# A graph attention layer on one core: slots of a word side by side, the maximum subtracted on VectorE, one exponent for four heads

## The reference

```
xl, xr = (h @ Wl), (h @ Wr)                      # (1250, 4, 64), h = rms(layernorm(x)) @ W_down
msg = xl[src] + xr[dst]
e = einsum(where(msg > 0, msg, 0.2 * msg), att)  # one number for each edge and head
m = segment_max(e, dst); p = exp(e - m[dst])
alpha = p / (segment_sum(p, dst) + 1e-16)
out = segment_sum(alpha * xl[src], dst) @ W_up
```

## Time and profile before

| what | value |
|---|---|
| three runs | 1125.25 us median (1120.89 to 1125.56) |
| the profiled execution | 1124.86 us, span 1122.3 us |
| mean granted TensorE clock | 0.931 |
| busy: PE, DVE, POOL, ACT | 970.0, 956.2, 616.1, 528.2 us |
| moved by transfers | 105.30 MB, 94 GB/s |

### The profile page before, as it was taken

One profiled execution on the slowest core, in us unless ns is written; L12 is line 12 of the kernel. 1 busy time (PEld: TensorE's weight loads), 2 busy tenths in 40 slices (PEclk: granted clock), 3 DMA queues, 4 the chain that ended last, 5 costly groups with the idle time before them and its releaser, 6 DMA issues.

```text
span 1122.3 us, 10318 instructions
## 1 busy us (share of the span) xinstructions
PE 970.0 (86%) x2998; PEld 465.6 (41%) x2998; DVE 956.2 (85%) x1078; ACT 528.2 (47%) x1901; POOL 616.1 (55%) x657
## 2 busy tenths in 40 slices
PE   0798999999999998999999999998999947566754
PEld 0675544444574343444344444443444423222321
DVE  6989648492999999999999999899997387888795
ACT  0123213311666677667878878767776121111111
POOL 2323327446666666676777777767762264444332
PEclk9899999999969999999999999998999967867788
DMA  8104051244343432553355333573320100000001
GB/s 255 76 1 119 10 181 34 51 142 139 100 155 80 155 83 77 158 160 98 87 156 171 84 82 91 208 280 81 91 79 22 61 1 0 38 19 19 20 37 52
DMA packets 59462, 105.30 MB, mean 94 GB/s; under 512 B 24631, under 2 KB 32468, under 8 KB 59130
## 3 DMA queue, kind: packets, MB, share of 16 engines
q0 software_dynamic: 18560, 50.70, 16.2%
q1 hardware_dynamic: 40842, 53.92, 14.4%
HBM read 92.30 MB, written 12.45 MB: 93 GB/s over the span
## 4 chain that ended last, share of the span: by engine, by line
DVE 48%; PE 32%; issue 10%; POOL 4%; SPq 2%; ACT 1%; DMA 1%; POOLq 0%; DVEq 0%; ACTq 0%
PE acc L715 25%; DVE acc_sb L1428 11%; DVE z L1558 7%; DVE round_mem L1556 7%; DVE round_mem L1419 4%; PE acc L888 3%; DVE round_mem L1174 3%; DVE round_mem L1175 2%; DVE round_mem L1173 2%; POOL round_mem L666 2%; PE acc L886 2%; POOL round_mem L490 1%; DVE round_mem L1172 1%; DVE big_b L1496 1%; DVE big_b L1372 1%
## 5 line engine op out<-in xcount | busy, mean ns | idle before, releaser
L666 POOL DMA_INDIRECT round_mem<-msg_table,idx x352 | 338.0, 960 | 99.9 <-issue 88.8
L1109 ACT ACTIVATE round_mem<-round_mem,pz 128x66 f32<-128x66 f32 x1408 | 345.1, 336 | 2.0
L715 PE MATMUL acc<-wslot,big_a 128*128 128x512 f32 x512 | 225.1, 600 | 4.4 <-issue 2.1
L1428 DVE TENSOR_REDUCE acc_sb<-round_mem 128x264 f32<-128x1848 f32 (+1 forms) x62 | 206.2, 3326 | 5.9 <-ACT round_mem L1109 3.8
L490 POOL TENSOR_TENSOR round_mem<-round_mem 128x1024 bf16<-128x1024 bf16 (+3 forms) x52 | 85.6, 1653 | 132.6 <-DVE round_mem L1176 87.7
L715 PEld LDWEIGHTS acc<-wslot,big_a 128*128 128x128 f32 x512 | 97.9, 193 | 127.5 <-issue 123.1
L715 PE MATMUL acc<-big_a,xhat_t 128*128 128x512 f32 x320 | 139.9, 600 | 6.5 <-ACT xhat_t L1039 5.0
L1102 ACT ACTIVATE pz<-z 128x7 f32<-128x7 f32 (+1 forms) x248 | 55.5, 296 | 148.3 <-DVE z L1565 105.7
L1419 DVE TENSOR_TENSOR round_mem<-round_mem,tp 128x1536 f32<-128x1536 f32 (+1 forms) x62 | 103.4, 1668 | 25.3 <-issue 19.8
L715 PE MATMUL acc<-wslot,big_b 128*128 128x512 f32 x256 | 113.1, 601 | 8.9 <-DVE big_a L1375 6.3
L715 PE MATMUL acc<-big_b,wslot 128*128 128x512 f32 x256 | 110.0, 592 | 0.0
(11 more groups left out here) (195 smaller groups left out, 1159.7 us busy)
## 6 DMA issues: line engine op xcount, KB each, us to landing
big_b<-in_x SPq DMA_DIRECT2D x18, 512.0 KB, 10.9
round_mem<-msg_table,idx POOLq DMA_INDIRECT x352
out_x<-big_b SPq DMA_DIRECT2D x9, 512.0 KB
wslot<-in_wv_t SPq DMA_DIRECT2D x2, 2048.0 KB
wslot<-in_wk_t SPq DMA_DIRECT2D x2, 2048.0 KB
wslot<-in_wo_t SPq DMA_DIRECT2D x2, 2048.0 KB
wslot<-in_wq SPq DMA_DIRECT2D x2, 2048.0 KB
wslot<-in_gate_w SPq DMA_DIRECT2D x1, 2048.0 KB
```

The costliest lines, as they stand in the source:

```text
L666: pool.indirect_dma_start(xg[g % 4][:, j, :], None, msg_table, bass.IndirectOffsetOnAxis(idx[:, c, j0 + j:j0 + j + 1], 0)).then_inc(xg_in[ ...
L715: mm = nc.tensor.matmul(o(acc[:, n % 4, :]), a, b, start=first, stop=last)
L1109: ins = nc.scalar.activation(xg[g % 4][:, j, cols], xg[g % 4][:, j, cols], ACT.Copy, scale=pz[:, g % 2, j, h:h + 1])
L1428: nc.vector.tensor_reduce(acc_sb[:, c, :], xg[g % 4][:, 0:n + 1, :].rearrange("p j f -> p f j"), AX.X, ALU.add).then_inc(sum_done, 1)
```

## The change

- **Weighted slots in an own buffer.** `round_mem` loses one slot of each `xg` buffer and `beside`, `msum`; it gains three half buffers (`weighted`, `halves_of`), in which a word's slots stand side by side. ACT's multiplications and POOL's `rescale` write there with a step of 7 words; `close` reads it in one piece. A round needs two of the three halves, so ACT waits between heads 1 and 2 for `sum_done` of the round before.
- **65 words for a head.** The linear part becomes word 0 of a head in `msg_table` and in `xr_sb`, so that adding the receiver adds it too and one sum over 65 words gives the score. `complete` on POOL, `beside`, `lin_done` and DVE's L1560 go. Slots that a node doesn't have now gather the row `NOBODY`, whose linear part is large (`far_col`).
- **PSUM.** `m4` lies in PSUM (`turned`, over four banks); the receiver is copied there by DVE at the first round of a chunk (`receiver`); `att` is read from SBUF. `show_receivers` and its waits go.
- **The maximum.** DVE subtracts the new maximum from the round's scores, and ACT takes one `Exp` over all slots and heads.
- **Order.** `gather(0)` is issued between pieces; `rescale(g - 3)` stands after the fourth gather of round g; a gather waits for `mul_done` only. Piece 11 is turned after `("p", 3)`. DVE enters the rounds on `wq_taken` 12 and not on the stores; those are waited for by ACT and POOL in round 0. The planner's clock becomes `268.0, 8.4`.

```diff
-ROUND_0_AT, ROUND_STEP = 286.0, 9.6
+ROUND_0_AT, ROUND_STEP = 268.0, 8.4
-                ("gram", 15): 8, ("p", 1): 9, ("p", 2): 10, ("p", 4): 11}
+                ("gram", 15): 8, ("p", 1): 9, ("p", 2): 10, ("p", 3): 11}
...
+        xg = [round_mem[0:NC, i * R * ROW:(i + 1) * R * ROW].rearrange("p (j f) -> p j f", j=R) for i in range(4)]
+        weighted = round_mem[0:NC, 4 * R * ROW:].rearrange("p (i f j) -> p i f j", i=3, j=R + 1)
+        halves_of = [weighted[:, 0:2], weighted[:, 2::-2], weighted[:, 1:3]]
...
+        turned = ps("turned", [P, 4 * HALF])
+        receiver = turned[0:NC, 0:H * MR].rearrange("p (h d) -> p h d", d=MR)
+        m4 = turned[0:NC, 4 * HALF - R * H * MR:].rearrange("p (j h d) -> p j h d", j=R, d=MR)
...
+            def gather(g):
+                c, j0, n, _, _ = ROUNDS[g]
+                if g >= 4:
+                    pool.wait_ge(mul_done, g - 3)
+                for j in range(n):
+                    if j == 4 and g >= 3:
+                        rescale(g - 3)
+                    pool.indirect_dma_start(xg[g % 4][:, j, :], None, msg_table,
+                                            bass.IndirectOffsetOnAxis(idx[:, c, j0 + j:j0 + j + 1], 0)).then_inc(xg_in[g % 4], 16)
...
+                    if q == 10:
+                        pool.wait_ge(idx_done, 1)
+                        pool.wait_ge(table_out, 16)
+                        gather(0)
                     leave_piece(q)
...
-        early = {index_of["p", i]: 273.0 + 3 * i for i in range(3)}
+        early = {index_of["p", i]: 257.0 + 2 * i for i in range(3)}
...
                 act.wait_ge(z_done, g + 1)
-                if first and 1 <= c < C - 1:
-                    show_receivers(c + 1)
+                nc.scalar.activation(pz[:, g % 2, 0:slots + 1, :], z[:, g % 3, 0:slots + 1, :], ACT.Exp, scale=-1.0).then_inc(e_done, 1)
+                act.wait_ge(e_done, g + 1)
                 for h in range(H):
-                    ins = nc.scalar.activation(pz[:, g % 2, 0:slots + 1, h], z[:, g % 3, 0:slots + 1, h], ACT.Exp, scale=-1.0,
-                                               bias=z[:, (g + 1) % 3, top_slot(g + 1), h:h + 1])
+                    if h == H // 2:
+                        if g >= 1:
+                            act.wait_ge(sum_done, g)
...
+                    to = halves_of[g % 3][:, h // 2, (h % 2) * MR:(h % 2 + 1) * MR, :]
+                    for j in range(slots):
+                        ins = nc.scalar.activation(to[:, :, j], xg[g % 4][:, j, h * HR + 1:(h + 1) * HR], ACT.Copy, scale=pz[:, g % 2, j, h:h + 1])
                 ins.then_inc(mul_done, 1)
...
-                nc.vector.tensor_reduce(acc_sb[:, c, :], xg[g % 4][:, 0:n + 1, :].rearrange("p j f -> p f j"), AX.X, ALU.add).then_inc(sum_done, 1)
+                nc.vector.tensor_reduce(running[c].rearrange("p (i f) -> p i f", i=2), halves_of[g % 3][:, :, :, 0:n + 1], AX.X,
+                                        ALU.add).then_inc(sum_done, 1)
...
-            for w in wt_out:
-                dve.wait_ge(w, 16 * 6)
+            dve.wait_ge(wq_taken, 12)
...
-                nc.vector.tensor_reduce(top, zz[:, 0:slots + 1].rearrange("p j h -> p h j"), AX.X, ALU.min).then_inc(z_done, 1)
+                step(nc.vector.tensor_reduce(top, zz[:, 0:slots + 1].rearrange("p j h -> p h j"), AX.X, ALU.min))
+                nc.vector.tensor_tensor(zz[:, 0:slots + 1], zz[:, 0:slots + 1], top.unsqueeze(1).to_broadcast([NC, slots + 1, H]),
+                                        ALU.subtract).then_inc(z_done, 1)
```

More of the change, by code:

```diff
@@ L288, in gps_layer @@
         gnn_out = [xr_sb[:, c, 0:HID] for c in range(C)]
-        xr_ps = [tp[0:NC, c % 2, 0:HID] for c in range(C)]
-        att_ps = tpb[0:NC, 0, 0:2 * HID].bitcast(F32)
+        running = [acc_sb[:, c, 0:H * MR] for c in range(C)]
         gnn_nat = [acc_sb[:, c, 0:HID] for c in range(C)]
```

145 lines of the change are left out of this document (56 added, 89 removed).

## The result

| what | before | changed |
|---|---|---|
| 20 runs each, beside each other | 1125.55 us median (1120.89 to 1130.78) | 1129.49 us median (1123.18 to 1133.85) |
| profiled execution | 1124.86 us, span 1122.3 | 1129.47 us, span 1127.3 |
| busy from 240 to 880: PE, DVE, ACT | 616.9, 586.6, 432.5 us | 614.7, 512.9, 398.0 us |
| rounds entered | 280.35 | 278.05 |
| last product of PE ends | 877.9 | 882.7 |

The ratio is 1.0041, 95% interval 1.0025 to 1.0056: a little slower. The forecast was 1125.0, faster or no change rather than slower. Later executions of the same changed kernel were far slower still (medians of 1159 to 1165 us); the experiments come to that.

The account below looks back on a forecast made before the run. PE bounds, following DVE's rounds up to its last gap: round 35 at 566, product taken at 569.5, 44 groups of 7.0 us end at 877.7, with the tail untouched 1125 us; range 1108 to 1146.

Parts of the forecast that it names:

- a 6-slot round: DVE's instructions for one round without a product: from 9.21 us to 7.87.
- PSUM at nothing: DVE reading and writing `m4` in PSUM: no added time; upper bound +1.2 us for each of three instructions.
- ACT didn't pace: Rival, chance 0.14: ACT's stepped multiplications pace the rounds from 0.31 us each; at 0.33 the time is 1140 us.
- the start: Between weight pieces and rounds: earlier first gathers, PE waiting 6.0 us for piece 10, rounds begun at 269.8, not 280.35.
- the flag and the jump: DVE before the rounds: 0.8 us for the flag, the jump at the low end of 1.24 and 5.39 us.
- The last wait for `t1`: PE's last gap, before the eleventh `t1` group: ACT takes `t1` 6 in round 35, at 569.5 us.
- The 44 groups behind it: PE's groups after the last gap: 7.0 us each, 308 us, ending at 877.7.
- the two gates that I held equal: PE's waits for `t1` 6 (round 35) and `base` 4 (behind round 60): the same end within 1 us.
- none behind 570: PE's timeline: gaps of about 1.5 us in `kv` and early `t1`, and no gap after 570 us.
- 1119.5 to 1130.5: The range in us of the likeliest case, same time within 0.5%.
- the likeliest case: Same time within 0.5%, chance 0.40: the plan takes products in later rounds, so PE's gaps stay, 21.8 against 22.0 us.
- POOL's rival: Slower, chance 0.05: a stepped write makes `rescale` take twice its time, 8.7 us a round, 1135 us.

Follow-up runs that it names:

- e1: The changed kernel with the planner's two old numbers (286 and 9.6): 1122.87 us, 0.9986 of the kernel before.
- e15: The changed kernel with one gather less in each round from round 4 on and the old plan (286 and 9.6): 1109.55 us, 0.9899 of the kernel before.
- e4: The kernel before with the new plan (268 and 8.4), nothing else: 1202.89 us, 1.0709 of the kernel before.
- e14: The changed kernel with one gather less in each round from round 4 on, new plan: 1128.79 us, 1.0062 of the kernel before.
- e6: The changed kernel with unused slots gathering 30 different padding rows, not one: 1160.29 us, 1.0332 of the kernel before.
- e7: The changed kernel with unused slots spread over 30 rows and the old plan (286 and 9.6): 1125.73 us, 1.0032 of the kernel before.
- e13: The changed kernel unedited, the control of the fourth group: 1165.14 us, 1.0382 of the kernel before.
- e5: The changed kernel unedited, run again in the second group: 1160.37 us, 1.0353 of the kernel before.
- e12: The changed kernel with scaled messages laid slot after slot as before, not side by side: 1212.77 us, 1.0810 of the kernel before.
- e11: The kernel before with unused slots gathering the last row, one small DVE instruction more: 1122.07 us, 1.0001 of the kernel before.
- e16: The kernel before with one gather more in each round: 1193.06 us, 1.0629 of the kernel before.
- e3: The changed kernel with the first round's six gathers moved back behind the last two weight pieces: 1154.51 us, 1.0275 of the kernel before.

## Why the prediction was wrong

**Right, by its own steps.** `close` 2.05 and 1.78 us (forecast 2.05 and 1.78); a 6-slot round 7.85 (7.87); PSUM at nothing; the receiver's copy 0.43; ACT's cadence 0.25 and its one exponent 0.23, so ACT didn't pace; the wait for `sum_done` cost nothing, though ACT stood 39.8 us in it; PE bounds, and DVE's 74 us less are worth nothing behind the last gate. The subtraction, at 0.226 us, was 0.2. On PSUM: the sum (L1548) had no operand there before and takes 1783 ns for 1753, with 24 elements more, which at 1.04 ns make 25 of the 30. The Trainium skill (VectorE: DVE Perf Modes, The TRN2 errata) would by my sum have added 0.2 us a round, and the rows don't show it. That sum was too large in any case: it counted three instructions, and two of them had an operand in PSUM before.

**The step that failed is the start.** I had "first instruction of the rounds at 269.8", with 274 as the high end; it was 278.05. The 8.25 us are, within 0.1: the first gather 1.2 late (250.5 for 249.3); the six gathers 2.05 more (9.45 for 7.4), which I had priced from rows where DVE ran other work; PE's next group 1.7 and the turns 0.6 more at the lower clock, which I hadn't priced at all; and 2.8 in the flag and the jump, 4.9 us for the 2.1 that I took, at the low end of my two rows.

Put through my sum, that is the miss of the first runs, and it shows a second size that was off, the other way. The last wait for `t1` should have ended at about 569.5 and ended at 577.0, 7.5 later. The 44 groups behind it took 302.5 us and not 308, since a group that waits for nothing takes 6.88 us (110.1 for the last 16) and not my 7.0. And of the two gates that I held equal within a microsecond, `base` 4 was the later one, by 3.2 us, so "none behind 570" fell: 577.0 + 302.5 + 3.2 = 882.7, for 877.7. That 1129.5 lies inside my 1119.5 to 1130.5 is thus partly luck: with the right price of a group I would have said some 1119.5, and missed by 10. The sign, slower, is the start's and the gate's.

**The mechanism held.** A group waits for a round that the plan names, and the new plan names later ones. I had said so and taken it as the likeliest case, but left the old plan aside as a comparison. With 286 and 9.6 and the short rounds, e1's expectation had no gap but piece 10's and an end at 868 to 870; e15, with a sixth of the gathers missing, shows just that, at 859.6. The new numbers cost the long rounds 78 us (e4) and the short ones 19 (e14 to e15) to 35 (e6 to e7). So what the shorter rounds save goes into the new plan, and nothing is left over.

**What no step held: the crawls, and a stop of ACT.** POOL's rival had a chance of 0.05 for a slow `rescale`, which was wrong in kind. The gathers did become the limit, but through PE and ACT: e13 to e14, with a sixth of the gathers left out, is 36 us. Between the first runs (1129.5) and e5 (1160.4) lie 31 us, and 4 of them are something else. In round 1 ACT's exponent is done at 292.7 in e5, and its multiplications start at 298.2:

```profile
292.50 0.23 ACT L1092 ACTIVATE pz<-z 128x28 f32<-128x28 f32 x1 [0.98 <-issue]
298.18 4.01 ACT L1103 ACTIVATE round_mem<-round_mem,pz 128x65 f32<-128x65 f32 x16 [5.45 <-remote]
```

DVE (4.51 us) and POOL (2.86) stand with it, the first `close` comes at 298.2 and not at 294.1, and p0 begins at 318.1 and not at 314.1. At the same place DVE and POOL stand until 295.5 to 300 in all fifteen later traces of the changed kernel and its variants, e12, e14 and e15 among them, which have no crawl. The changed kernel's first trace lacks it, and so do the kernel before, e4, e11 and e16. What ACT waits for there isn't shown.

**Open.** The first runs of the changed kernel (20, median 1129.5) have no crawl in their trace, though POOL issues 75 gathers from 272 to 372 and 146 from 543 to 748 with no pause over 0.8 us there, more in a row than in any trace that crawls, and p0 takes 24.3 us:

```profile
314.11 24.30 PE L717 MATMUL acc<-colsum,wslot 128*128 128x1 f32 x128 [0.76 <-DVE big_b L1366]
```

The same kernel crawled in each of three later groups, each on another chip. So dense gathers go with the crawls in every pair that I ran, but something else, which no run here shows, decides whether they come. It could be the chip, or where things lay in its memory; that is a guess, and no run here tests it. The stop of ACT in round 1 sets the first trace apart from the later ones too, crawls or not. What PE and ACT wait for in them isn't shown either. Nor is the start taken by itself: e3 moves it, with crawls on top. A version faster than both that leaves nothing out wasn't found; e1 (0.9986, its interval holds 1) is the nearest.

## What to carry to other kernels

Where work is placed by a table of due times, put the old table through with the new prices before costing a change: a shorter round with later places can lose, and here the places were worth 19 to 35 us, and the start with the last gate 5. Look at the last gate, not at the busiest engine. When an engine that used to pause in a round becomes nearly continuous, its own instructions may stay the same and the others' issue may not. And repeat the control in every group: this kernel read 1129, 1160, 1159 and 1165.

## What the hardware showed that I had not expected

- Gathers beside DVE's work. Four gathers took 1.27 to 1.65 us and two 0.95. DVE ran the scaling of a piece meanwhile; the long gather at 252.09 lies over these two:

```profile
251.69 1.23 DVE L1168 SCALAR_TENSOR_TENSOR wslot<-round_mem,wslot 128x1024 f32<-128x1024 f32 x1
252.95 1.22 DVE L1169 SCALAR_TENSOR_TENSOR round_mem<-round_mem,wslot 128x1024 bf16<-128x1024 f32 x1
```

  The Trainium skill (SBUF — State Buffer, the note on DVE blocking DMAs from GpSimd) says that an instruction of DVE in a two-port mode locks GpSimd out of a shared port while it writes its descriptors. It agrees only in part: the gathers of 1.27 and 1.44 us lie over the one-input L1166 and L1167, which take 0.69 us for 1024 elements and so may be of that kind, but the two of 1.65 lie over the two-input instructions shown, which the note doesn't name. No run here isolates it.
- Crawls: 0.70 us a start and its multiples, on PE and on ACT, in all 12 later profiled executions with all gathers and the short rounds, and in e16, and in none of e4, e11, e12, e14, e15 and the kernel before.
- Many descriptors for one row of DRAM: packets of 4224 bytes averaged 558 ns between 325 and 345 in the changed kernel, 228 in the kernel before and 237 in e6, where the rows are spread. It moved no time here: e6 is within 0.1 us of e5.
- A stepped write made ACT's row 62 ns longer (336 to 398) and its cadence not at all.
- The granted clock fell to its lower level inside a gap of 7.6 us of PE and stayed there 6.8 us. Short gaps went both ways: at the end of one of 2.47 us (e3) and one of 2.19 us (e16) it fell for 3.4 us, over one of 2.17 us (the kernel before) and one of 2.94 us (e11) it stayed up.
- In p0 PE goes on without a gap, but on products of one column, and the granted clock falls all the same: its mean is 1.00 from 310 to 315, 0.75 from 315 to 320 and 0.50 from 320 to 340 in the changed kernel. The starts go from 0.11 to 0.21 us apart, so most of p0's 24.3 us is spent at the lower level.
